# One core, a scan mixer and a quantised feed-forward block: the second layer norm of all eight tiles on VectorE, the rounding scale of six tiles on GpSimd, and new instruction orders

## The reference

```python
# block 1: for each sequence (b) and channel (d), a state of 16 numbers (n)
u = silu(conv4(in_proj(ctx)) + conv_b)                 # 256 channels
dt = softplus(dt_proj(dt_low) + b);  B, C = x_proj(u)
state = state * exp(dt * A) + (dt * u) * B             # over 256 tokens
y = (sum_n state * C + D * u) * silu(layernorm(x))
x = x + y
# block 2
h = silu(bitlinear(layernorm(x), w1, b1))              # 256 -> 1024
h = gelu(h, approximate=False)
h = (h - mean) * rsqrt(var + EPS) * ln_g + ln_b        # second layer norm, over 1024
x = x + bitlinear(h, w2, b2)                           # 1024 -> 256
# bitlinear: rms_norm, row scaled by 127/absmax and rounded; weights rounded to -1, 0, 1
```

## Time and profile before

| | us |
|---|---|
| time, median of 3 runs | 200.37 (200.09 to 201.26) |
| profiled execution: time | 200.04 |
| profiled execution: span | 198.1 |
| VectorE busy | 167.5 (85%) |
| ScalarE busy | 161.1 (81%) |
| TensorE busy (matmul) | 159.7 (81%) |
| GpSimd busy | 127.8 (65%) |

### The profile page before, as it was taken

How to read it: one execution, slowest core, us unless ns; L and a number is a source line. 1 busy time by engine, 2 the same in 40 slices (tenths; PEclk the granted TensorE clock), 3 DMA queues, 4 the chain that set the end, 5 groups by cost and what they waited for, 6 DMA issues and landing times.

```text
span 198.1 us, 3315 instructions
## 1 busy us (share of the span) xinstructions
PE 159.7 (81%) x1161; PEld 118.8 (60%) x1167; DVE 167.5 (85%) x225; ACT 161.1 (81%) x255; POOL 127.8 (65%) x117
## 2 busy tenths in 40 slices
...
GB/s 136 341 4 332 388 418 271 4 73 322 229 28 129 86 60 55 206 109 23 195 0 85 132 100 115 0 28 0 0 3 0 26 0 0 0 30 26 3 39 67
DMA packets 20192, 20.12 MB, mean 102 GB/s; under 512 B 13448, under 2 KB 16976, under 8 KB 19536
## 3 DMA queue, kind: packets, MB, share of 16 engines
...
q10 hardware_dynamic: 592, 0.77, 1.4%
HBM read 17.70 MB, written 2.21 MB: 101 GB/s over the span
## 4 chain that ended last, share of the span: by engine, by line
DVE 33%; PE 29%; issue 16%; POOL 10%; ACT 8%; DMA 2%; DVEq 0%; POOLq 0%; ACTq 0%
DVE st L956 13%; PE ps L517 9%; PE ps L555 5%; PE ps L454 4%; POOL st L829 4%; DVE stats L1026 4%; ACT dA L681 3%; DVE xc L991 3%; DVE am L1051 3%; PE ps L483 3%; PE ps L432 2%; DMA inw_sb<-inwT 2%; POOL w_raw L891 2%; DVE w_raw L963 2%; PE ps L465 2%
## 5 line engine op out<-in xcount | busy, mean ns | idle before, releaser
L829 POOL TENSOR_TENSOR st<-st,bc 128x1024 f32<-128x1024 f32 x32 | 77.5, 2437 | 27.8 <-DVE st L956 27.6
L956 DVE TENSOR_TENSOR_SCAN st<-dA,ps 128x1024 f32<-128x1024 f32 x32 | 71.7, 2271 | 8.6 <-PE ps L517 7.3
L681 ACT ACTIVATE dA<-dt,negA 128x255 f32<-128x255 f32 x128 | 52.7, 494 | 0.6 <-POOL negA L810 0.6
L517 PE MATMUL ps<-diagB,dtuT 64*128 64x128 f32 x512 | 44.5, 307 | 10.6 <-DVE st L956 9.8
L517 PEld LDWEIGHTS ps<-diagB,dtuT 64*128 64x128 f32 x512 | 35.1, 202 | 22.8 <-DVE st L956 12.5
L778 ACT ACT_TABLE_LOAD x29 | 37.2, 1283 | 0.5
L555 PE MATMUL ps<-id_f,st 128*128 128x128 f32 x256 | 34.9, 288 | 2.7 <-POOL st L829 2.7
L555 PEld LDWEIGHTS ps<-id_f,st 128*128 128x128 f32 x256 | 30.5, 149 | 5.9 <-POOL st L829 3.9
L592 PE MATMUL ps<-rows_sb,diag 128*128 128x512 f32 x32 | 17.2, 664 | 1.8 <-ACT q2T L750 1.2
L616 PE MATMUL ps<-id_f,w_raw 128*128 128x128 f32 x64 | 10.7, 322 | 9.1 <-POOL w_raw L891 6.8
L616 PEld LDWEIGHTS ps<-id_f,w_raw 128*128 128x128 f32 x64 | 8.6, 165 | 11.3 <-issue 11.0
...
## 6 DMA issues: line engine op xcount, KB each, us to landing
...
```

Of the source, the lines that this page charges most:

```text
L517: mm = nc.tensor.matmul(o[:, i:i + SG // 2, t, r, :], dtuT[rows, b % 2, h, t, :], diagB[rows, b % 2, t, n, :], start=True, stop=True)
L681: e = nc.scalar.activation(dA[:, k % DA_RING, i * L + 1:(i + 1) * L], dt[:, h, b, 1:L], ACT.Exp, scale=negA[:, h, n:n + 1])
L829: tt(s, s, bc[:, ng].rearrange("p s l -> p (s l)"), ALU.mult).then_inc(prod_done, 1)
L956: nc.vector.tensor_tensor_scan(st[:, k % ST_RING, :], dA[:, k % DA_RING, :], slot(k), 0.0, ALU.mult, ALU.add).then_inc(scanned, 1)
```

## The change

`norm` of tiles 0 to 3 leaves ScalarE, `shift` of tiles 0 to 3 leaves GpSimd, and `gain` of tiles 0 to 3 becomes the pair L1036 and L1040 on VectorE. `scale2` stays on ScalarE for tiles 0 and 1; tiles 2 and 3 get `scale_last` on GpSimd. The third instruction of `root2a` (L858) goes. All four tables are written anew, and the semaphore counts follow. Two tuples name the kinds:

```diff
+NORM_BY_SCALAR = (())
+SCALE_BY_SCALAR = (0,1)
@@ VECTOR_AT: all rows new, of which two
-    "clip_weights:0",
+    "clip_weights:0 quant1:0 clip_weights:1",
...
+        def nth(t, kind):
+            return sum(q in kind for q in range(t + 1))
         def root2a_before(t):
-            return 3 * min(t, LAST) + 2 * max(t - LAST, 0)
+            return 2 * t + sum(q in NORM_BY_SCALAR for q in range(t))
         def norm_of(t):
-            return (norm_done, t + 1) if t < LAST else (shifted_last, t - LAST + 1)
+            return (norm_done, nth(t, NORM_BY_SCALAR)) if t in NORM_BY_SCALAR else (shifted_last, t + 1 - nth(t, NORM_BY_SCALAR))
         def w_of(t):
-            return (w_done, t + 1) if t < LAST else (w_last, t - LAST + 1)
+            return (w_done, nth(t, SCALE_BY_SCALAR)) if t in SCALE_BY_SCALAR else (w_last, t + 1 - nth(t, SCALE_BY_SCALAR))
...
             def root2a(t):
...
-                if t < LAST:
-                    pool.wait_ge(root2a_step, 3 * t + 2)
+                if t in NORM_BY_SCALAR:
+                    pool.wait_ge(root2a_step, root2a_before(t) + 2)
                     ts(s[:, 2:3], mv2[:, t % 2, 0:1], s[:, 1:2], -1.0, ALU.mult, ALU.mult).then_inc(root2a_step, 1)
...
             def gain(t):
                 h = hid[:, t % HSLOTS]
-                if t >= LAST:
+                if t not in NORM_BY_SCALAR:
                     dve.wait_ge(mv2_done, t + 1)
...
-                dve.wait_ge(norm_done, t + 1)
+                dve.wait_ge(*norm_of(t))
```

More of the change, by code:

```diff
@@ L54 @@
 VECTOR_AT = (
-    "spread_b:1 z_norm:1 times_half:1 spread_b:2 spread_b:3",
+    "spread_b:1 z_norm:1 spread_b:2 times_half:1 spread_b:3",
+    "",
     "",
@@ L59 @@
     "",
-    "wmean:0",
     "",
     "",
-    "clip_weights:0",
+    "wmean:0",
+    "times_u:2",
+    "",
+    "gate:0 gate:1 x1:0 x1:1 ln1:0",
+    "",
+    "clip_weights:0 quant1:0 clip_weights:1",
     "",
     "",
-    "gate:0 gate:1 x1:0 x1:1 times_u:2 ln1:0",
     "",
-    "quant1:0",
+    "bn2:0",
+    "gain:0 times_u:3 gate:2",
+    "gate:3 amax2:0 x1:2 x1:3 bn2:1 ln1:1 scales2:0 quant1:1 gain:1",
     "",
     "",
-    "times_u:3 clip_weights:1",
     "",
-    "gate:2 x1:2 bn2:0 gate:3",
+    "amax2:1",
     "",
-    "x1:3 ln1:1 gain:0",
-    "bn2:1",
-    "quant1:1",
+    "scales2:1",
+    "bn2:2 gate:4 gate:5",
+    "x1:4 x1:5",
+    "ln1:2 gain:2 quant1:2 amax2:2 res:0 scales2:2",
     "",
-    "amax2:0 scales2:0 gain:1",
     "",
[L81 to L89, removed]
+    "bn2:3",
+    "gain:3 res:1 gate:6 gate:7 x1:6 amax2:3 x1:7 scales2:3 ln1:3 res:2 quant1:3 bn2:4 bn2:5 gain:4 gain:5 "
+    "amax2:4 bn2:6 scales2:4 amax2:5 gain:6 bn2:7 scales2:5 amax2:6 res:3 gain:7 scales2:6 res:4 amax2:7 "
+    "scales2:7 res:5 res:6 res:7",
 )
@@ L96 @@
     "",
[L97 to L101, removed]
-    "",
-    "",
-    "delta:2 silu_u:3 copy_z:0",
+    "silu_u:1 silu_z:0 silu_u:2 copy_xd:1 delta:1",
+    "copy_half:1",
+    "",
+    "",
+    "sum_weights:0 copy_xd:2 sum_weights:1 copy_du:1",
+    "",
+    "delta:2 silu_z:1 copy_z:0 scale_weights:0 silu_u:3",
     "copy_xd:3",
@@ L108 @@
     "",
+    "scale_weights:1 delta:3",
+    "copy_q1:0",
+    "silu:0 silu_z:2 gelu:0 copy_z:1",
+    "",
+    "silu:1 square:0 silu_z:3 gelu:1 copy_du:3",
+    "",
+    "copy_z:2",
+    "",
+    "copy_z:3 square:1 copy_q1:1",
     "",
     "",
-    "delta:3 scale_weights:1 silu_z:1 copy_q1:0 silu_z:2 silu_z:3 copy_z:1 silu:0 gelu:0",
     "",
-    "copy_du:3",
-    "norm:0 silu:1 gelu:1 copy_z:2",
+    "silu:2 gelu:2",
     "",
-    "copy_z:3 square:0 norm:1 copy_q1:1",
+    "scale2:0",
     "",
[L118 to L125, removed]
+    "copy_q2:0 scale2:1 silu:3 square:2 copy_q2:1 gelu:3 copy_q1:2 copy_q2:2 silu:4 square:3 silu:5 gelu:4 "
+    "copy_q2:3 gelu:5 copy_q1:3 silu:6 gelu:6 square:4 silu:7 square:5 gelu:7 square:6 copy_q2:4 square:7 "
+    "copy_q2:5 copy_q2:6 copy_q2:7",
 )
@@ L144 @@
     "",
+    "root2a:0 root2b:0",
     "",
-    "root2a:0",
+    "root1:1 out_scale:0 root2a:1 root2b:1 add_b2:1",
     "",
-    "root1:1 shift:0",
-    "root2a:1",
-    "root2b:0",
-    "",
[L152 to L156, removed]
+    "",
+    "",
+    "",
+    "",
+    "root2a:2",
+    "",
+    "out_scale:1 root1:2 root2b:2",
+    "scale_last:2",
+    "",
+    "",
     "root2a:3",
[L158 to L161, removed]
+    "add_b2:2 root2b:3 out_scale:2 scale_last:3 root1:3 out_scale:3 root2a:4 root2a:5 root2b:4 out_scale:4 "
+    "add_b2:3 root2a:6 scale_last:4 root2b:5 root2b:6 root2a:7 scale_last:5 out_scale:5 scale_last:6 root2b:7 "
     "scale_last:7 out_scale:6 out_scale:7",
@@ L170 @@
-    "scale_b:7 scale_rest:7",
-    "dtraw:2 scale_b:8 scale_b:9 scale_rest:8 scale_rest:9",
-    "",
-    "convolve:7 scale_b:10 scale_rest:10 turn_z:0",
-    "scale_b:11 scale_rest:11 scale_b:12 xdbl:3",
+    "scale_b:8 scale_b:9 scale_rest:8 dtraw:2",
+    "scale_rest:9",
+    "turn_z:0 scale_b:10 scale_rest:10 convolve:7 scale_b:11 scale_rest:11 scale_b:12 scale_rest:12 xdbl:3",
+    "turn_du:2 dtraw:3 scale_b:13 scale_b:14 scale_rest:13",
+    "",
+    "scale_rest:14",
     "",
+    "turn_q1:0 bias:0 mm1:0 scale_b:15 scale_rest:15 scale_b:16 turn_z:1 scale_rest:16",
@@ L189 @@
[L189 to L199 removed]
+    "scale_b:17 scale_b:18 scale_rest:17 scale_rest:18 bias:1 mm1:1 scale_b:19",
```

42 lines of the change are left out of this document (21 added, 21 removed).

## The result

| | before | after |
|---|---|---|
| time, median of 4 runs each, same chip | 200.23 (200.08 to 201.26) | 191.61 (190.36 to 191.99) |
| profiled execution: time, span | 200.04, 198.1 | 191.23, 189.2 |

The ratio is 0.9548, with a 95% interval of 0.9491 to 0.9606. The change takes away 8.6 us by the medians and 9.1 by the ratio; 5.6 had been forecast.

A forecast was written before the change was run, and what follows sets the result against it. VectorE was taken to bound the kernel, partly by waiting for GpSimd's products. Scan 31 ending at 149.3 plus tail 36.0 plus last chain 7.6 gave span 192.9, with 1.94 around it 194.8 us; own range 192 to 198, whole 190.0 to 202.5.

The forecast's parts named there:

- scan 8 starts: Start of the middle stretch: estimated at 49.3 us, between 46.5 (nothing late) and 51.5.
- middle: other work of VectorE: Middle stretch, VectorE work that isn't scans or waiting: 33.4 becomes 39.1 us with longer norms and clip_weights:0 moved in.
- middle: waits for products: Middle stretch, VectorE held by GpSimd's running products: 5.0 us instead of 12.7, bounds 2 and 14.8.
- middle: idle: Middle stretch, VectorE's gaps: 2.6 us before, minus 0.5 because exponentials and products are ready earlier, so 2.1.
- tail: After scan 31, before the last chain: 34.9 plus 2.6 of gain:3, covering about 1.5 of idle: 36.0 us.
- the 1.4 for the rest: Middle stretch: product waits left beside 2.1 for the clips and 1.5 for times_u:2, within the 5.0 us.
- The pairs: L1036 and L1040 on VectorE, tiles 0 to 2: zero hold by products, which stand behind root2b; 2.56 us each pair.
- wrong if L1040 has a mean over 1.6: Sign against the forecast: L1036 or L1040 averaging over 1.6 us, where 1.28 with a count of eight each was expected.
- It is cover: ScalarE's 11 us and GpSimd's 5 us of relief count at nothing directly; only 0.5 us of late scans goes.
- A: Rival, slower: every kind of VectorE work stays held by products, waits 14.8 instead of 5.0, 204.6 us; chance 0.12.
- B: Rival, no change: GpSimd's products queued behind root2b:1 and root2b:2 start 4 to 5 us late, 199.3 us; chance 0.14.
- C: Rival, better: waits 2.0, scan 8 at 48.3, tail idle 2.3, thanks to ScalarE's 11 us; 190.3 us, chance 0.14.

The follow-up runs named there:

- experiment 4: Changed kernel with root2b of tiles 0, 1 and 2 one product later in GpSimd's list, beside the pairs; 196.85 us, ratio 0.9843.
- experiment 5: Kernel before with each GpSimd product cut from 1024 to 8 columns; 187.27 us, ratio 0.934.
- experiment 6: Changed kernel with each GpSimd product cut to 8 columns; 190.38 us, ratio 0.9492 to the kernel before.
- Experiment 7: Changed kernel with nine added ScalarE instructions into a spare buffer, 11 us in all; 200.07 us, ratio 0.9964 to the kernel before.
- experiment 1: Kernel before, its orders kept, with only the short norm for tiles 0 to 3 (pair L1036, L1040 on VectorE); 205.14 us, ratio 1.0238.
- experiment 2: Changed kernel's orders, with the second norm of tiles 0 to 3 again in three parts; 209.05 us, ratio 1.0428 to the kernel before.

## Why the prediction was right, and where its sizes were off

**Direction and mechanism.** The forecast was 194.8 us and faster; it came to 191.6, below the forecast's own range of 192 to 198 and inside the whole one. The mechanism it named, waits of VectorE for running products, is what experiments 4 to 6 show: put back at three pairs they cost 5.0 us, and taken away from the kernel before they give 13.4.

**The sum, term by term.**

| term | forecast | profile after |
|---|---|---|
| scan 8 starts | 49.3 | 48.0 |
| middle: scans | 53.8 | 53.9 |
| middle: other work of VectorE | 39.1 | 37.7 |
| middle: waits for products | 5.0 | 2.1 |
| middle: idle | 2.1 | 3.3 |
| tail | 36.0 | 36.6 |
| last chain | 7.6 | 7.6 |
| span | 192.9 | 189.2 |

*Waits, the mis-sized term.* The one wait for the clips came, 3.27 - 1.23 = 2.0 where 2.1 was forecast. The 1.5 for `times_u:2` and the 1.4 for the rest did not come: L930 has a mean of 672 ns, L991, L1012 and L1009 are bare. For most of them the step's own reason (a gate or statistics ahead, or GpSimd waiting) held. For L930 at 50.21 it was another: GpSimd's last product had ended at 48.06 and its next began at 50.43, behind L930, so the product was the one held (two took 5.14 us instead of 4.67).

*Other work.* 37.7 is busy 93.66 less scans and the 2.1. I had taken L963's 1.63 at 48.25 as free; experiment 5 shows 1.21. That is 0.4 too much in the work carried over and again in the clip added, 0.8 of the 1.4; the rest is not placed.

*The start.* 0.9 of the 1.3 is no effect of the change: this execution reached its first scan at 20.39 us instead of 21.27, while VectorE's first wait for an input was 6.39 us instead of 6.98; two kernels with the orders of the change had their first scan at 20.8 (experiments 6 and 7), one with those of before at 20.48 (experiment 5), so this start differs from run to run. L1089 was held for some 2 us at 45.80 (2.29 for two columns) at next to no cost: in experiment 6, where it took 0.15, scan 8 waited 1.83 us for TensorE instead and started 0.2 sooner, counted from the first scan.

*The pairs.* Zero hold for tiles 0 to 2 was right, for the reason given (L1040 mean 1284 there). For `gain:3` I counted 2.6 and no hold, though the last product starts at that moment: it took 1.26 + 3.19. By the Trainium skill, "SBUF — State Buffer", section "Who interferes with whom", a VectorE instruction with two SBUF inputs contends with a GpSimd instruction that reads SBUF, and the one that issues second is blocked until the first is through. The trace agrees: 3.19 against 1.28 beside the product at 145.21, and so do the rows of experiment 4. The tail's idle time fell to 36.6 - 35.0 = 1.6 where 2.8 was forecast, which hid most of it.

*My test "wrong if L1040 has a mean over 1.6" came true* (1679 ns over eight) while the forecast's reason stood. The mean mixed three held instructions of the tail (3.19, 1.95, 1.87) with five free ones. The test belonged to the middle stretch alone.

**"It is cover", the step that failed.** I counted the relief of ScalarE and GpSimd "at nothing directly". Experiment 7 puts 11 us back on ScalarE and loses 8.5 by the medians, 8.3 by the ratios. With VectorE at 97% and ScalarE at 87% of the stretch before, the gain on the first was not to be had without the relief of the second. The number came out since the real change brings both, and since errors of both signs met: the middle's idle time (1.2 more than forecast) and the tail (0.6 more) took back part of what the waits, the other work and the start gave (2.9, 1.4 and 1.3 less). Asked for the parts alone, I had the norm right (experiment 1: 203 expected, 205.1 measured) and the orders wrong by 18 us (experiment 2). What GpSimd's relief is worth no run shows.

**The rivals.** A's limit of 10.2 us counts from the profiled execution (200.04 less 194.8); from the median, as the forecast of 5.6 does, it is 10.6. A (waits stay, pairs held) is out for this order, but is what experiments 1 and 4 show for others. B (GpSimd's queue): the engine did stand 13.0 us in the middle before `root2b` for the squares (4.21 + 4.75 + 3.99), and scans still waited only 2.5 us there, so the buffers covered it. C (190.3: waits 2.0, scan 8 at 48.3, tail idle 2.3) came nearest, and its reason, ScalarE's 11 us, had been undervalued by me.
